# First attention takes its tokens by sequences from inside its loop, behind a TensorE warm-up

## The reference, cut to what matters

```python
x = x + _L0_xattn_ref(_layernorm(x), ctx, lens, W_q, W_k, W_v, W_o)   # this case
x = x + _L0_ffn_ref(_layernorm(x), ...)                               # shared + top 2 of 8 experts
...                                                                   # three more such pairs

def _L0_xattn_ref(queries, keys, sequence_length, W_q, W_k, W_v, W_o):
    B, L, D, H = (4, 256, 128, 8)
    Q = (queries @ W_q.T).reshape(b, lq, H, DH).transpose(2, 0, 1, 3)
    K = (keys @ W_k.T).reshape(b, lk, H, DH).transpose(2, 0, 1, 3)
    V = (keys @ W_v.T).reshape(b, lk, H, DH).transpose(2, 0, 1, 3)
    scores = jnp.einsum('hbqd,hbkd->hbqk', Q, K) / jnp.sqrt(jnp.float32(DH))
    key_mask = jnp.arange(lk)[None, :] < sequence_length[:, None]
    scores = jnp.where(key_mask[None, :, None, :], scores, NEG)
    attn = jax.nn.softmax(scores, axis=-1)
    q_mask = (jnp.arange(lq)[None, :] < sequence_length[:, None])
    attn = attn * q_mask[None, :, :, None]
    out = jnp.einsum('hbqk,hbkd->hbqd', attn, V)
    return out.transpose(1, 2, 0, 3).reshape(b, lq, d) @ W_o.T
```

## Time and profile before

| | |
|---|---|
| time, median of 3 runs | 775.22 us (772.02 to 777.85) |
| the profiled execution | 779.8 us, span 777.9 us |
| PE busy, share of the span | 638.7 us, 82% |
| DVE busy | 417.3 us, 54% |
| ACT busy | 374.0 us, 48% |
| POOL busy | 199.7 us, 26% |
| DMA queue of SP and ACT | 82.98 MB, 39.3% of 16 engines' span |

### The profile page before, as it was taken

The page is one execution under the profiler, slowest core; times in us unless marked ns, Lnnn a source line. Parts: engine busy times, 40 slices in busy tenths (PEclk is TensorE's granted clock), DMA queues, the critical chain, the costliest instruction groups (busy, mean ns, idle before and its releaser), DMA issues.

```text
span 777.9 us, 14428 instructions
## 1 busy us (share of the span) xinstructions
PE 638.7 (82%) x4792; PEld 492.4 (63%) x4792; DVE 417.3 (54%) x1426; ACT 374.0 (48%) x939; POOL 199.7 (26%) x372
## 2 busy tenths in 40 slices
PE   5498678999898997857987879986979777986895
PEld 2165478877565665656877656763969734544894
DVE  5776631424246569844533787681423577883412
ACT  5265233555264454764544455653323325755553
POOL 2224521030022002131331151123223143222335
PEclk9699578999999999997998999997899988999998
DMA  7797097010288775020176513324026432441140
GB/s 234 182 281 297 25 197 165 29 38 17 93 212 236 260 214 157 8 72 14 35 193 104 134 50 93 113 90 96 27 83 177 101 90 66 138 144 59 42 113 28
DMA packets 105972, 91.51 MB, mean 118 GB/s; under 512 B 11667, under 2 KB 97177, under 8 KB 105901
## 3 DMA queue, kind: packets, MB, share of 16 engines
q1 hardware_dynamic: 101964, 82.98, 39.3%
q0 software_dynamic: 3936, 7.62, 3.6%
HBM read 53.52 MB, written 36.31 MB: 115 GB/s over the span
## 4 chain that ended last, share of the span: by engine, by line
PE 59%; DVE 16%; issue 7%; ACT 6%; POOL 5%; another core or an unknown queue 4%; DMA 2%; POOLq 0%; DVEq 0%; SPq 0%; ACTq 0%
PE bank L1978 12%; PE bank L1999 10%; PE bank L1816 5%; PE bank L1799 4%; PE bank L1764 4%; PE bank L2076 2%; DVE negmax L953 2%; PE bank L2109 2%; PE bank L1955 2%; PE bank L1938 2%; PE bank L1913 2%; DVE xn L807 2%; PE bank L1927 2%; DVE stats L797 2%
## 5 line engine op out<-in xcount | busy, mean ns | idle before, releaser
L1999 PE MATMUL bank<-W,spare 128*128 128x128 f32 (+1 forms) x960 | 134.5, 285 | 19.3 <-ACT spare L1564 9.1
L1999 PEld LDWEIGHTS bank<-W,spare 128*128 128x128 f32 x960 | 122.9, 200 | 23.2 <-issue 10.4
L1479 ACT ACTIVATE late<-bank 128x512 f32<-128x512 f32 x120 | 70.8, 594 | 56.8 <-PE bank L1804 26.4
L953 DVE TENSOR_REDUCE negmax<-bank 128x2 f32<-128x512 f32 x128 | 85.3, 688 | 22.6 <-PE bank L1764 17.2
L1564 ACT ACTIVATE spare<-bank,W 128x128 f32<-128x128 f32 x224 | 63.4, 372 | 56.1 <-PE bank L1978 43.1
L671 POOL DMA_INDIRECT rows_sorted<-xn,idx x56 | 55.9, 999 | 96.9 <-DVE idx L1031 82.3
L1764 PE MATMUL bank<-big 128*128 128x256 bf16 x320 | 68.7, 289 | 14.1 <-DVE negmax L953 13.0
L1799 PE MATMUL bank<-big 128*128 128x256 bf16 x320 | 74.0, 282 | 5.1 <-issue 4.6
L1612 ACT ACTIVATE big<-big,r 128x256 f32<-128x256 f32 x64 | 31.9, 500 | 47.8 <-DVE r L1300 41.9
L1764 PEld LDWEIGHTS bank<-big 128*128 128x128 bf16 x320 | 27.6, 102 | 38.5 <-DVE negmax L953 24.6
L1816 PE MATMUL bank<-late 128*32 128x256 f32 x480 | 46.0, 410 | 0.1
(11 more groups left out here) (289 smaller groups left out, 1375.1 us busy)
## 6 DMA issues: line engine op xcount, KB each, us to landing
W<-in_f_wx SPq DMA_DIRECT2D x25, 578.0 KB, 7.0
late<-bands_scratch SPq DMA_DIRECT2D x8, 1024.0 KB, 5.8
W<-in_f_wx SPq DMA_DIRECT2D x8, 514.0 KB, 3.5
big<-parts_scratch SPq DMA_DIRECT2D x4, 768.0 KB, 7.0
bands_scratch<-zrow SPq DMA_DIRECT2D x4, 768.0 KB
big<-parts_scratch SPq DMA_DIRECT2D x12, 256.0 KB, 3.9
stage<-rows_sorted SPq DMA_DIRECT2D x11, 256.0 KB
rows_sorted<-stage SPq DMA_DIRECT2D x9, 256.0 KB, 3.2
```

The source lines that it names most:

```text
L953: ins = v.tensor_reduce(negmax[:, g % 2, :, j], bank[i % 2][:, :].rearrange("p (t k) -> p t k", t=2), AX.X, ALU.max, negate=True)
L1479: a.activation(PTs[j % NPT][:, :, :], bank[2 + j % 2][:, :].rearrange("p (c q) -> p c q", c=2), ACT.Exp)\
L1999: ins = mm(dst[:, 128 * place_:128 * (place_ + 1)], hidB[n % 3][:, c, :], w2[:, 128 * c:128 * (c + 1)], start=c == 0, stop=c == FC - 1)
```

## The change

In a0 the queries now come in four parts of one sequence each, as in a2 and a3. The first two are turned, projected and split ahead of the loop, the last two in it: `LATER["a0"]` is {2: 1, 3: 5}, so that their statistics are made at steps 1 and 5, their normalisation at 2 and 6, turn and queries at 4 and 8, their split at 6 and 10. The values' copies go to step 4, the second half of the mask row to step 7, `masks` to step 9. The loop's first scores wait for the first key half, the first sequence's queries, and the mask row of the first half.

SP's order becomes: x in three loads, mask row half 0, key stack 0, query stacks 0 and 1, key stack 1, the eight small loads, query stack 2, mask row half 1, query stack 3, the later weights of the attentions, clears, experts. The two context loads and the lengths are issued by ACT. The fills on ACT are cut in halves. The parts of a0's queries lie in the room of experts 0 and 1 (`W`), whose loads therefore wait for the last two query stacks.

`stack_out` and `stack_in` become one `stack`, in all three narrow attentions: write, wait for the write, read, with nothing between. The keys of a2 and a3 are written in two halves, each just ahead of its read, and the split of the queries waits for the landing of the key half. Each run of writes waits only for the parts that it sends.

PE makes 16 transposes of the identity before its first product. The values of a0 and two of its turns use other PSUM banks.

```diff
-LATER = {2: 14, 3: 21}
+LATER = {"a0": {2: 1, 3: 5}, "a2": {2: 14, 3: 21}, "a3": {2: 14, 3: 21}}
...
-        parts0 = spare[:, :].bitcast(bf16).rearrange("p (c t) -> p c t", c=3)
+        parts0 = W[:, 0:2, :].rearrange("p e c -> p (e c)")[:, 0:1536].bitcast(bf16).rearrange("p (c t) -> p c t", c=3)
...
+            def stack(key, side, p):
 
                 H, d, _ = NARROW[key]
+                cols = slice(512 * p, 512 * (p + 1)) if side else piece(key, p)
+                src = parts if side or key != "a0" else parts0
+                n = 3 * p if key == "a0" or not side else 0
...
+                for first, many, part in ((0, 3, 0), (3, 2, 1), (5, 1, 2)) if not side else ((0, 3, None), (3, 2, None), (5, 1, 0)):
+                    sp.wait_ge(*at(key, "kp" if side else "qp", n + (3 if side else part + 1)))
+                    rows_ = src[:, 0:many, cols] if part is None else \
+                        src[:, part:part + 1, cols].broadcast_to([128, many, cols.stop - cols.start])
+                    sp.dma_start(scratch[side, first:first + many, :, cols].rearrange("r p t -> p r t"), rows_).then_inc(sem("st.w"), 16)
+                    writes[0] += 16
+                sp.wait_ge(sem("st.w"), writes[0])
+                by_head = scratch[side].rearrange("r (i h) t -> (r i) h t", h=H)
                 for row, r0, r1 in STACK_ROWS[key]:
+                    sp.dma_start((Qs, Ks)[side][row:row + (r1 - r0) * d, 0:H, cols], by_head[r0 * d:r1 * d, :, cols])\
+                      .then_inc((keys_landed if side else landed)(key, p)[0], 16)
...
-            stack_out("a0", 1, 0)
-            stack_out("a0", 0, 0)
-            stack_in("a0", 1, 0)
-            stack_in("a0", 0, 0)
-            sp.wait_ge(sem("c.mask"), 1)
-            sp.dma_start(Ks[MASK_ROW:MASK_ROW + 1, 1:8, :], Ks[MASK_ROW:MASK_ROW + 1, 0:1, :].broadcast_to([1, 7, TOK]))\
-              .then_inc(sem("ld.mask"), 16)
-            sp.wait_ge(*landed("a0", 0))
-            stack_out("a0", 1, 1)
-            stack_out("a0", 0, 1)
-            stack_in("a0", 1, 1)
-            stack_in("a0", 0, 1)
+            mask_to_heads(0)
+            stack("a0", 1, 0)
+            stack("a0", 0, 0)
+            stack("a0", 0, 1)
+            stack("a0", 1, 1)
+            for dst, src in small:
+                sp.dma_start(dst, src).then_inc(sem("ld.small"), 16)
+            stack("a0", 0, 2)
+            mask_to_heads(1)
+            stack("a0", 0, 3)
+            sp.dma_start(aw[:, 4:12, :], A["aw"][4:12].rearrange("w i o -> i w o")).then_inc(sem("ld.aw2"), 16)
...
             expert("f0", 8)
+            sp.wait_ge(*landed("a0", 2))
+            sp.wait_ge(*landed("a0", 3))
             for e in range(8):
                 expert("f0", e)
...
             def attention_transfers(key, before, nxt):
 
-                stack_in(key, 1, 1)
+                stack(key, 1, 1)
                 stack(key, 0, 0)
                 y_out(before, 1, 2)
-                stack_out(key, 0, 1)
+                stack(key, 0, 1)
                 y_out(before, 1, 3)
-                stack_in(key, 0, 1)
...
                 if key == "a0":
-                    x_ready(dve, key, 0)
+                    dve.wait_ge(sem("ld.x0"), 16)
                     norm_stats(key, 0, x)
+                    mask_row(0)
                     norm_apply(key, 0, x, xn)
+                    dve.wait_ge(sem("ld.x1"), 16)
+                    norm_stats(key, 1, x)
                     dve.wait_ge(*at(key, "kt", 1))
-                    split(KT, slice(0, 512), "kp")
+                    split(KT, slice(0, 512), key, "kp", 0)
+                    norm_apply(key, 1, x, xn)
                     query_parts(key, 0)
+                    query_parts(key, 1)
                     dve.wait_ge(*at(key, "kt", 2))
-                    split(KT, slice(512, TOK), "kp")
-                    x_ready(dve, key, 1)
-                    norm_stats(key, 1, x)
-                    norm_apply(key, 1, x, xn)
-                    mask_row()
-                    values(key)
-                    query_parts(key, 1)
-                    masks()
+                    split(KT, slice(512, TOK), key, "kp", 1)
...
+                    if key == "a0":
+                        if i == 4:
+                            values(key)
+                        if i == 7:
+                            mask_row(1)
+                        if i == 9:
+                            masks()
...
             pe.wait_ge(sem("c.const"), 1)
+            for i in range(16):
+                tr(bank[i % 2][:, 0:128], ident[:, :], ident[:, :])
             pe.wait_ge(sem("ld.qk"), 16)
...
                 if key == "a0":
                     keys(key, (0,))
-                    turn_norm(key, 0)
-                    queries(key, 0)
+                    for hf in range(2):
+                        turn_norm(key, hf)
+                        queries(key, hf)
                     keys(key, (1,))
                     values(key)
-                    turn_norm(key, 1)
-                    queries(key, 1)
...
-                    if h == 0 and (b % 2 == 0 or key != "a0"):
-                        pe.wait_ge(*landed(key, b // 2 if key == "a0" else b))
+                    if h == 0:
+                        pe.wait_ge(*landed(key, b))
                     if h == 0 and b == 2:
-                        pe.wait_ge(sem("st.k1"), 16 + 32 * LAYER_OF[key])
+                        pe.wait_ge(*keys_landed(key, 1))
```

More of the change, by code:

```diff
@@ L411, in stack_in @@
-            def stack_in(key, side, half=None):
-                H, d, _ = NARROW[key]
-                cols = piece(key, half)
-                if side:
-                    cols = slice(512 * half, 512 * (half + 1))
-                dst = (Qs, Ks)[side]
-                if key == "a2":
-                    sp.wait_ge(sem("c.zero"), 16)
-                sp.wait_ge(*written(key, side, half))
-                src = scratch[side].rearrange("r (i h) t -> (r i) h t", h=H)
-                for row, r0, r1 in STACK_ROWS[key]:
-                    sp.dma_start(dst[row:row + (r1 - r0) * d, 0:H, cols], src[r0 * d:r1 * d, :, cols])\
-                      .then_inc(sem(f"st.k{half}") if side else landed(key, half)[0], 16)
@@ L963, in attention @@
                     late_half = key != "a0"
-                    for hf, start in LATER.items() if late_half else ():
-                        if i == start - 4 and hf == 2:
+                    if key == "a0":
[5 more added lines that the diff above has]
+                            masks()
+                    for hf, start in LATER[key].items():
+                        if late_half and i == start - 4 and hf == 2:
                             weights(BEFORE[key], 1)
-                        if i == start:
+                        if i == start and not late_half:
+                            dve.wait_ge(sem("ld.x2"), 16)
+                            norm_stats(key, hf, x)
+                        elif i == start:
                             combine(BEFORE[key], 1, (2 * hf - 4, 2 * hf - 3))
@@ L1411, in queries @@
                 cols = piece(key, hf)
-                qt, src = QT[:, cols], bank[M[int(key != "a0" and hf < 2 or hf == 0)]][:, 0:cols.stop - cols.start]
+                qt, src = QT[:, cols], bank[M[int(hf < 2)]][:, 0:cols.stop - cols.start]
                 if key == "a3":
@@ L1483, in attention @@
                         act.wait_ge(*at(key, "pv", 4 * g + 4))
-                        if key == "a0" and g == 0:
-                            act.wait_ge(*written("a0", 0, 1))
                         if g >= 2:
@@ L1718, in values @@
                 for c in range(2):
-                    dst = take(M[c])
+                    k = (PVB if key == "a0" else M)[c]
+                    dst = take(k)
                     for i in range(4):
@@ L1795, in shifted @@
                         pe.wait_ge(sem("c.maddT"), 1)
+                    if key == "a0" and i == 0:
+                        pe.wait_ge(sem("c.const"), 4)
                     dst = take(2 + i % 2)
@@ L1864, in attention @@
                         out_project(b - 1)
-                    for hf, start in LATER.items() if key != "a0" else ():
+                    for hf, start in LATER[key].items():
                         if i == start + 3:
```

161 lines of the change are left out of this document (74 added, 87 removed).

## The result

| | before | after |
|---|---|---|
| time, median | 776.54 us (772.02 to 778.99, 4 runs) | 799.32 us (798.31 to 801.25, 4 runs) |
| the profiled execution, its span | 779.8 us, 777.9 us | 798.31 us, 796.4 us |
| mean granted clock of TensorE | 0.921 | 0.907 |

The ratio is 1.030, with a 95% interval of 1.025 to 1.036: slower by 23 us, where I had forecast 779.2 and a range up to 787. The profiled execution is 18.5 us longer.

A forecast was written before the change was run, and what follows sets the result against it. VectorE and the opening's hops were taken to bound the first twelve heads, TensorE the rest. 1.2 + 1.0 + 1.8 = plus 4.0 on the profiled 779.8 gave 783.8, less 4.6 for the runs' median 779.2 us; range 768 to 787.

The forecast's parts named there:

- the last sentence on the other two attentions: Second and third attention: halving the key write and waiting for the keys' landing precede work needed several us later, cost 0.
- the second of the signs: Forecast is wrong if the difference arises behind the first mixture, where none but the two stores was expected.
- The stores late: Third and second attention: result stores behind the query read delay the chain 1.5 and 0.3 us; plus 1.8 taken.
- The first attention: Opening and loop of a0: plus 1.2 us at the twelfth maximum, plus 1.0 for the clock.
- Key parts ready: Opening of a0: key parts ready at 10.6 us, bounds 10.1 to 11.3, against 11.05 before.
- The query writes: Opening of a0: first sequence's query writes land 2.4 us after issue, read issued at 18.8, landed at 23.7.
- The loop to the twelfth maximum: Loop of a0: 7.6 us for eleven heads, 9.6 of moved VectorE work, 1.0 of TensorE hold-ups.
- Other items in the loop have cover: Loop of a0: later stacks and small loads arrive before heads need them, with cover of 3 to 4 us.
- The clock: Dense part of a0's loop: TensorE may enter it at half clock; plus 1.0 us, bounds 0 and 4.3.
- the head start: Opening of a0: first maximum at 24.9 us against 32.96, 8.1 sooner, lost again to work moved into the loop.
- stacks late: Rival, first attention: head 16 or the masks wait for SP's stacks; plus 4.5 us, 784 us, chance 7%.
- the warm-up: Opening of a0: 16 transposes buy nothing for the loop, since TensorE idles from some 17 to 24 us; 0 taken.

The follow-up runs named there:

- e2: Changed kernel with only the keys of the second and third attention written whole before their first read again; ratio to before 1.024, 795 us at the expected base.
- e3: Changed kernel with the old SP order of the second and third attention back, except that keys stay written in halves; ratio to before 1.019.
- e1: Changed kernel with the old SP order of the second and third attention back, first attention still changed; ratio to before 1.015.
- e12: As e3, but key half 1 written right behind the read of half 0, and half 0 one transfer ahead of its read; ratio to before 1.011.
- e10: Changed kernel with only the store of the feed-forward's last pieces put back before the read of query sequence 1, second and third attention; ratio to before 1.028.
- e8: Kernel before with only the store of the feed-forward's last pieces moved behind the read of query sequence 1; 0.7% slower, 5 us by ratio (1.7 to 8.7).
- e6: e5 with the first attention's sequence 0 query writes on their own semaphore, issued before the key read; ratio to before 1.007.
- e5: e1 with the first attention's eight small loads issued before the first key write; ratio to before 1.008.
- e4: Changed kernel without the 16 warm-up transposes; time level with after, first attention ending 0.3 us earlier.
- e7: As e6, but ScalarE issues the first attention's read of key half 0 on its own queue; ratio to before 1.002.

## Why the prediction was wrong

**The step that failed** is the last sentence on the other two attentions: "Splitting the key write in two halves, and waiting for the keys' landing instead of their write, lies before work that comes several us later: 0". e2 and e3 measured 8 to 12 us for it over both attentions by the steps, 3 to 5 by the whole times. The half of the sentence on the keys' landing held: e1 keeps that wait, and its steps are -0.1 and -1.9. The halving's did not. I asked who uses key half 1, the scores of the third sequence, and not who stands behind it on SP. Its write now waits for two stores of the mixture, its read for its write, and the first queries, which the whole loop waits for, have the read in front of them. e12 shows that it is the place of the writes and not the halving. With this came the second of the signs that I had named for being wrong, a difference that arises behind the first mixture.

**The stores late**: taken at 1.8, bounds 0 and 3.4. Measured together with the maxima's place 7 to 11, of the store alone 2.0 + 2.6 by the steps of e10 and 5 by e8's ratio. The mechanism was right and the size was off, on two counts: the store is delayed by a write's landing that itself takes 3.4 us in the second attention (444.05; I had 2.0), and beside POOL's fetch, ScalarE waits for this store before its first copy in the loop, which I had not looked up. The maxima of groups 4 and 6 behind a read I had not priced at all; whether they cost anything is open.

**The first attention**: taken at +1.2 and +1.0 for the clock, measured +5.5. Its steps one by one:
- Key parts ready 10.6, measured 10.45; key read issued 14.2, measured 14.16. Right.
- The query writes: landing 2.4, measured 4.8, behind a key read as above (issued ahead of that read, in e6, both reads followed at once); then the read 4.9, measured 4.2 (21.39 to 25.61, TensorE's first score). First maximum 24.9, measured 26.23: 1.3 late.
- The loop to the twelfth maximum: 7.6 + 9.6 + 1.0 = 18.2, measured 19.2, of which 2.35 is the wait for the small loads. "Other items in the loop have cover" held for the heads but not for the masks. Without that wait it is 16.8, 1.4 under my count; the moved work was sized well enough.
- The clock: taken 1.0, measured 2.0 (+3.5 to +5.5). It fell behind that same wait, and without the wait it did not fall (e5); but with the wait the seven profiles give 0 to 2.0, so this term of the changed kernel is in part chance.

VectorE's ledger answers the earlier trace rows: it is busy 12.26 + 15.06 = 27.3 us before the twelfth maximum, 27.0 then.

```profile
0.00:26.23 26.23, 12.26 (x34) 0.76 0.55 155
26.23:45.40 19.17, 15.06 (x48) 0.59 0.67 177
```

The moved work does take the head start away, as I argued, but most of the loss that is left in the first attention is again what stands in front of what on SP: e5 and e6 take 6.6 us off e1's +4.9, of which up to 1.3 is the clock, so that this attention ends 1.7 us before the old one.

**The sum**: 5.5 + 6.8 + 10.0 = 22.3 against the forecast 4.0; the profiled executions differ by 18.5, since the shift fell by 3.8 us net between the steps, in code that is unchanged. Of the rivals, "stacks late" had the mechanism with 7%, in the first attention only, and 4.5 us.

The Trainium skill (TensorE: Matmul & The Clock Gate, HAM oscillation) says that an array which idles for a transfer falls back to half rate. The traces agree: with the warm-up (after) and without it (e4), TensorE waits for the stacks up to 25.6 us and is granted 0.50 from 24 to 40, and the warm-up bought nothing for the loop that these runs can tell, as the forecast said.

## What to carry to other kernels

When a write, a wait and a read are joined into one step on a queue, price each for what is queued behind it, not for who needs its data: data needed late can still delay data needed now. A small write that a loop waits for should be issued before a large read and never just behind it; here this was worth 3.6 us in one place (e6); in two others together, with the wait for the key write, 8 to 12 us by the steps and 3 to 5 by the whole times. And look for every engine that waits for a store which is moved, the head of the loop of each included.

## What the runs showed of the hardware

- A landing depends on what was issued before it. The three writes of one query stack (128 x 3, 2 and 1 x 256 bf16, 384 KB) landed 1.3 to 1.5 us after the end of their issue in the second attention where the key read of 768 KB had been issued 5.1 to 6.3 us before them (before, e1, e2, e12), and 4.9 to 5.1 us after it where it had been issued 1.3 us before them (after, e3, e4, e10). In the third attention the landing took 5.1 us with the read 1.3 us ahead (e10), 3.9 with 2.3 to 2.5 (after, e3), 2.1 to 2.9 with 4.3 (e1, e2, e12) and 1.3 with 5.9 (before). In all of these but the short ones of 1.3 to 1.5 the writes were known to have landed 7.9 to 8.9 us after the start of the read's issue, and the page of before has 7.0 us for the landing of a read of 768 KB: they landed about when the read did, or a little later. In the first attention it was 4.8 us behind a key read, and 5.1 (e6) and 5.2 (e7) behind a key read and a query read; in e7 the key read was on another engine's queue. The Trainium skill (DMA: Bandwidth & Descriptors, Queues, rings and completion order) says that the queues of SP and ScalarE are rings on the same 16 engines, and that a semaphore's increment lands only after every earlier write of the same DMA engine, across its queues. The runs agree with this, but transfers that only share the bandwidth could look alike; no run here had the writes alone on their queue behind the read, which would show it by itself.
- A wait of 2.00 to 2.35 us of VectorE in the loop was followed by a granted clock of 0.57 to 0.79 from 44 to 52 us in five profiles (after, e1, e2, e4, e10) and of 1.00 in two (e3, e12), all with the same first attention but for e4's missing warm-up; without the wait it was 1.00 in this stretch (e5). A single profile does not tell what such a wait costs: here 0 to 2 us beyond itself.
